# Layer-norm in three parts, gate copies between weight splits, and ScalarE weighing the last heads

## The chip, the cores and the metric

The kernel runs on one core of one Trainium2 chip. The metric is the device time in microseconds of one execution. Three runs of the kernel before gave 857.67, 858.05 and 861.17 us, so the median is 858.05 us.

## What is computed

`x` is 4 x 256 tokens of 512 numbers. The reference, cut to what matters:

```python
xn = _layernorm(x, axis=-1)                      # (x - mean) / sqrt(var + 1e-5)
s = _L0_attn_ref(xn, wq, wk, wv, wo)             # 32 query heads, 8 key heads, head 128, window 128, rope
g = _silu(_L0_ffn_ref(xn, w1, s1, w2, s2, w3, s3))
x = x + s * g
# _L0_ffn_ref: weights are packed 4-bit numbers, one scale for 64 of them
a = einsum('bsd,hd->bsh', x, W1); b = einsum('bsd,hd->bsh', x, W3)      # hidden 1376
h = _silu(a) * b; return einsum('bsh,dh->bsd', h, W2)
# _L0_attn_ref, for each head: scores, mask, softmax, times v, then @ wo
```

## The kernel before

Every large product is made of three products of rounded parts: an operand `w` is split into a high part `wh` (a copy to the rounded type, by ScalarE) and a low part `wl = w - wh` (by VectorE or GpSimd), and `three` (L1005) adds `sh*mh`, `sh*ml` and `sl*mh` in one PSUM bank. Each engine runs a list written out by hand, in order; semaphores tie the lists together.

**Start.** SyncE issues the loads (L223 to L230): the first packed weights `load13(0, 0)`, then rows 0 to 3 of `x` (a row tile is 128 tokens x 512), then more weights, then rows 4 to 7. VectorE dequantises the first weights (`dequant13(0, 0)`: `nib`, a shift of the packed numbers, and `W13`, a product with the scales). It then takes `bn_stats` of four rows, and `scales(0)` turns them into a mean and a reciprocal root in seven small steps, with ScalarE's square root (`root`) between. `norm_here` (VectorE) and `norm` (ScalarE) normalise rows. TensorE first spreads the scales of the first weights over the partitions (`scale_rows`, L1069), then transposes the normalised rows (`x_turn`, L1018), which ScalarE (`x_hi`) and VectorE (`x_lo`) split. `w13_start` (L1042) computes the first hidden tile in quarter pieces of 256 tokens, `w13_mult` in pieces of 512. The low part of the first four weights is made by GpSimd (`w13_first`), and `x_turn(4)` to `x_turn(7)` run inside and after `w13_mult(1, 0, 0)`. The second four rows are normalised by `scales(1)`. `PARTS` (L176) holds the two parts.

**FFN.** There are 11 hidden tiles of 128, `t` = 0 to 10. For each, TensorE computes `a` and `b` for two halves of the tokens (`w13_tile`), ScalarE applies silu, VectorE multiplies (`hid`), and both split the result. After each odd tile from 3 on, `w2_mult(u)` computes the second product of tiles 2u and 2u+1 for 8 token tiles, in 4 PSUM banks used in turn; tile `i` waits until tile `i-4` has been read. The reader is VectorE's `ffn_add(u)`, which copies (u = 0) or adds each token tile into `gate`. In VectorE's list it stands at the end of iteration `t = 2u+3` (L806 to L811), behind `w13_lo(t + 2, 0)` and `w13_lo(t + 2, 1)`, the low parts of the weights two tiles ahead.

**Attention.** The eight key heads (`g`) and two pairs of batches (`bp`) make 16 steps. In a step four query heads of two batches (`b` = 0, 1) go through `scores` (TensorE), `masking` (VectorE, with the row maximum), `exps` (ScalarE, with the row sum), `inverse` (a reciprocal) and `normalise` (VectorE multiplies the probabilities by it, 128 and then 256 columns, L855), `p_turn` (TensorE transposes them), `p_hi` and `p_lo` (split), `attend`, `o_hi` and `o_lo`, and `out_project`. Each head is prepared in the step before the one that uses it.

**End.** In the last step but one (`last`, `bp == 0`), VectorE prepares the four heads of batch 0 for the last step (L973 to L983): `finish(0, 0)`, `masking`, four `normalise`, and `finish(0, 1)` in between. In the last step the heads of batch 1 follow: VectorE normalises head 0, ScalarE (`weigh`, L546) heads 1 to 3. TensorE's last step (L1202 to L1216) is `p_turn` 0 and 1, `out_project(g, 0, 3)`, `p_turn` 2, `attend(0)`, and so on. `finish(bp, t)` multiplies a projected tile with the gate. GpSimd meanwhile runs `rest(t)` (two operations for each of 8 tiles) and `add_rest(t)`, and SyncE stores the tiles.

Of the kernel before, what the change touches and what calls it, by code (L numbers as in the profile page):

```python
# [20 lines left out]
GH = NQ // NKV  # L21
# [5 lines left out]
NT = TOK // P  # L27
DT = D // P
# [16 lines left out]
def build(nc, x, wq, wk, wv, wo, w13, s13, w2, s2, const, shifts, side, out):  # L45
# [10 lines left out]
    with ctx:  # L56
# [118 lines left out]

        PARTS = ((0, 1, 2, 3), (4, 5, 6, 7))  # L176

# [26 lines left out]
        def _(sp):  # L204
# [13 lines left out]
            def load2(t):  # L218
                wait(sp, W2_done, t - 1)
                sp.dma_start(pk2[:, t % 2, :], w2[t]).then_inc(w2_in[t % 2], 16)  # L220
                sp.dma_start(sc2[:, t % 2, :], s2[t]).then_inc(w2_in[t % 2], 16)

            load13(0, 0)  # L223
            for i in range(4):
                load_x(i)
            load13(0, 1)
            load13(1, 0)
            for i in range(4, NT):
# [175 lines left out]
        def _(act):  # L404
# [47 lines left out]
            nc.scalar.activation(warm[:, 1:2], warm[:, 0:1], ACT.Sqrt)  # L452
            w13_hi(0, 0)
            root(0)
            norm(1)
            for i in range(4):
                x_hi(i)
            w13_hi(0, 1)
            w13_hi(1, 0)
            root(1)  # L460
            nc.scalar.activation(warm[:, 2:3], warm[:, 0:1], ACT.Silu)
            w13_hi(1, 1)
            norm(5)
            norm(7)
            x_hi(4)
            x_hi(5)
# [124 lines left out]
            def step(g, bp, last):  # L591
# [4 lines left out]
                if not more:  # L596
                    p_hi(g, bp, 0, 0)
                    p_hi(g, bp, 0, 1)
                    exps(g, bp, 1, 2)
                    exps(g, bp, 1, 3)  # L600
                    weigh(g, bp, 1, 1)
                    p_hi(g, bp, 0, 2)
                    weigh(g, bp, 1, 2)
                    weigh(g, bp, 1, 3)
                    o_hi(g, bp, 0)
                    o_hi(g, bp, 1)
                    for r in range(3):
                        p_hi(g, bp, 1, r)
                    o_hi(g, bp, 2)
                    o_hi(g, bp, 3)  # L610
                    return
# [31 lines left out]
                kq_hi(ng, nbp, 4)  # L643
                for h in range(GH):
                    exps(ng, nbp, 0, h)
                if last:
                    exps(ng, nbp, 1, 0)
                    exps(ng, nbp, 1, 1)
                if nxt:
                    for c in range(6):  # L650
                        hi_in(g + 1, c)
# [11 lines left out]
        def _(dve):  # L663
# [4 lines left out]

            def scales(part):

# [6 lines left out]
                v, r0, r, t = [std[:, n, first:last] for n in (0, 1, 2, 3)]  # L677
                nc.vector.tensor_scalar(v, mv[:, first:last, 1], EPS, None, ALU.add).then_inc(ln_small, 1)
                dve.wait_ge(std_done, part + 1)
                nc.vector.reciprocal(r, r0).then_inc(ln_small, 1)  # L680
# [22 lines left out]

            def dequant13(t, m):

                s = t % 2
                dve.wait_ge(w13_in[s][m], 64 * (t // 2) + 32)
                if t < 2:
                    dve.wait_ge(sfirst_ps, 2 * t + m + 1)
                if 1 <= t <= 2:  # L710
                    dve.wait_ge(W13l_first, 2 * t + m - 1)
                wait(dve, W13_done, 2 * t + m)
                nc.vector.tensor_scalar(nib[:, m, :], pk[:, s, m, :], shc[:, 4:5], shc[:, 5:6],  # L713
                                        ALU.logical_shift_left, ALU.arith_shift_right).then_inc(nib_done, 1)
                dve.wait_ge(nib_done, 2 * t + m + 1)
                scale = bank[2 + 2 * t + m][:, :] if t < 2 else sc[:, s, m, :]
                nc.vector.tensor_tensor(W13[:, m, :], nib[:, m, :], scale, ALU.mult).then_inc(W13_done, 1)

            def w13_lo(t, m):
# [38 lines left out]

            nc.vector.memset(warm[:, :], 1.0).then_inc(warm_set, 1)
            dve.wait_ge(shift_in, 16)  # L760
            dequant13(0, 0)
            for i in range(4):
                stats(i)
            scales(0)
            norm_here(0)
            norm_here(2)
            norm_here(3)
            x_lo(0)
            x_lo(1)
            dequant13(0, 1)  # L770
            x_lo(2)
            x_lo(3)
            dequant13(1, 0)
            for i in range(4, NT):
                stats(i)
            scales(1)
            norm_here(4)
            norm_here(6)
            dequant13(1, 1)
            x_lo(4)  # L780
# [16 lines left out]
            for t in range(2, FT):  # L797
                if t + 2 < FT:
                    dequant13(t + 2, 0)
                hid(t, 0)  # L800
                if t + 2 < FT:
                    dequant13(t + 2, 1)
                dequant2(t - 1 if t < FT - 1 else t)
                if t == FT - 2:
                    dequant2(t)
                hid(t, 1)  # L806
                if t + 2 < FT:
                    w13_lo(t + 2, 0)
                    w13_lo(t + 2, 1)
                if t > 2 and t % 2:  # L810
                    ffn_add((t - 3) // 2)  # L811
            def cos_part(g, bp, c):
# [105 lines left out]
            def step(g, bp, last):  # L918
                ng, nbp = (g, 1) if bp == 0 else (g + 1, 0)
                more = not (last and bp == 1)  # L920
                if not more:
                    p_lo(g, bp, 0, 0)
                    p_lo(g, bp, 0, 1)
                    normalise(g, bp, 1, 0)
                    inverse(g, bp, 1, 1)
                    finish(0, 2)
                    inverse(g, bp, 1, 2)
                    finish(0, 3)
                    inverse(g, bp, 1, 3)
                    p_lo(g, bp, 0, 2)  # L930
# [42 lines left out]
                if last:  # L973
                    finish(0, 0)
                    masking(ng, nbp, 0, 2)
                    normalise(ng, nbp, 0, 0)
                    normalise(ng, nbp, 0, 1)
                    masking(ng, nbp, 1, 0)
                    normalise(ng, nbp, 0, 2)
                    normalise(ng, nbp, 0, 3)  # L980
                    finish(0, 1)
                    masking(ng, nbp, 1, 2)
# [21 lines left out]
        def _(pe):  # L1004
# [13 lines left out]
            def x_turn(i):  # L1018
                if i in (1, 5, 7):
                    pe.wait_ge(xn_done, (1, 5, 7).index(i) + 1)  # L1020
                else:
                    pe.wait_ge(xn_here, (0, 2, 3, 4, 6).index(i) + 1)
                wait(pe, xl_done, i - 3)
# [17 lines left out]

            def w13_start(m, part):  # L1042

# [4 lines left out]
                          [(W13h[:, 0, m, d, :], W13l[:, 0, m, d, :], xh[:, d, cols], xl[:, d, cols])  # L1048
                           for d in range(DT)])
                if part:  # L1050
# [26 lines left out]
            pe.wait_ge(id_in, 16)  # L1077
            for i in range(4):
                x_turn(i)
            scale_rows(1, 0)  # L1080
            scale_rows(1, 1)
            w13_start(0, 0)
            w13_start(0, 1)
            w13_mult(0, 0, 1)
            w13_mult(1, 0, 0, {3: lambda: x_turn(4)})
            for i in range(5, NT):
                x_turn(i)
            w13_mult(1, 0, 1)
# [242 lines left out]
```

## Time and profile before

| what | us |
|---|---|
| median of three runs | 858.05 |
| the profiled execution | 861.75 |
| its span (first to last instruction) | 859.9 |
| TensorE busy (matmul) | 834.0, 97% |
| VectorE busy | 610.6, 71% |
| ScalarE busy | 459.8, 53% |
| GpSimd busy | 394.7, 46% |

The profiled execution took 1.85 us more than its span, and 3.7 us more than the median of the three runs. TensorE's granted clock was 0.994 of full speed on average over it. TensorE is busy nearly all the time, so what counts is where it is not, and where its clock is low. The chain of work that ended last is 88% TensorE and 5% VectorE.

### The profile page before, as it was taken

Reading aid. Unit: us, or ns where it says so; the run is one execution under the profiler, and the core shown is the slowest. Engines: PE = TensorE matmul, PEld = TensorE weight load, DVE = VectorE, ACT = ScalarE, POOL = GpSimd, SP = SyncE. Lnnn points to the kernel's source line nnn. Section 1 sums busy time; section 2 is a strip of 40 time slices with the busy share of each in tenths; the row PEclk is TensorE's granted clock in tenths of the full one; section 3 lists DMA queues with packets and bytes.
Section 4 is the critical chain, followed back from the end, with each engine's and each line's share of the span. In section 5 each row is a group of like instructions: output and inputs, shape, how many; then the busy total and the mean of one; then the engine's idle time right before and its main releaser. Section 6 shows DMA issues by size and latency. Waiting matters only on the chain.

```text
span 859.9 us, 13737 instructions
## 1 busy us (share of the span) xinstructions
PE 834.0 (97%) x4140; PEld 695.4 (81%) x4140; DVE 610.6 (71%) x1626; ACT 459.8 (53%) x1133; POOL 394.7 (46%) x304
## 2 busy tenths in 40 slices
PE   6998999999889999999999999999999999999987
PEld 3887888888668888888888888888888888888865
DVE  6586667644678768785867687687858676876894
ACT  3431311313675747574855757475748557674842
POOL 1231312326365517453543655174535436641893
PEclk9999999999999999999999999999999999999989
DMA  7543322212012001201020120012010201200121
GB/s 209 159 120 101 104 74 69 63 48 74 2 49 69 7 1 50 74 2 36 13 73 0 49 63 10 0 49 73 0 34 15 73 0 49 63 10 1 49 63 74
DMA packets 43449, 44.48 MB, mean 52 GB/s; under 512 B 3476, under 2 KB 28182, under 8 KB 43414
## 3 DMA queue, kind: packets, MB, share of 16 engines
q1 hardware_dynamic: 43120, 43.99, 17.8%
q8 instruction: 17, 0.28, 0.1%
q14 instruction: 16, 0.13, 0.1%
q10 hardware_dynamic: 296, 0.09, 0.0%
HBM read 41.96 MB, written 2.10 MB: 51 GB/s over the span
## 4 chain that ended last, share of the span: by engine, by line
PE 88%; DVE 5%; issue 2%; ACT 2%; POOL 1%; DMA 0%; ACTq 0%; POOLq 0%; DVEq 0%
PE bank L1012 26%; PE bank L1014 26%; PE bank L1013 26%; PE bank L1148 5%; PE bank L1128 3%; DVE probs L855 1%; POOL acc L354 1%; PE bank L1118 1%; DVE W13l L721 1%; PE bank L1071 1%; PE bank L1025 1%; DVE nib L713 0%; DVE nib L737 0%; DVE act_h L730 0%; DVE probs L840 0%
## 5 line engine op out<-in xcount | busy, mean ns | idle before, releaser
L337 POOL TENSOR_TENSOR swap<-swap,cst 128x512 f32<-128x512 f32 x80 | 103.5, 1294 | 256.3 <-ACT swap L515 255.0
L1012 PE MATMUL bank<-xh,wih 128*128 128x512 f32 x384 | 158.0, 412 | 0.2 <-DVE q L819 0.2
L1014 PE MATMUL bank<-xh,wil 128*128 128x512 f32 x384 | 150.8, 393 | 0.0
L1013 PE MATMUL bank<-xl,wih 128*128 128x512 f32 x384 | 150.0, 391 | 0.0
L542 ACT ACTIVATE probs<-probs,nmx 128x128 f32<-128x128 f32 (+1 forms) x256 | 113.5, 445 | 36.6 <-DVE nmx L840 36.2
L855 DVE TENSOR_SCALAR probs<-probs,rinv 128x128 f32<-128x128 f32 x250 | 125.3, 543 | 4.4
L558 ACT ACTIVATE ph<-bank 128x512 fp32r<-128x512 f32 x96 | 55.7, 598 | 109.3 <-PE bank L1148 107.9
L1012 PE MATMUL bank<-woh,oh 128*128 128x512 f32 x256 | 101.0, 395 | 0.0
L1014 PE MATMUL bank<-woh,ol 128*128 128x512 f32 x256 | 100.5, 393 | 0.0
L1013 PE MATMUL bank<-wol,oh 128*128 128x512 f32 x256 | 100.5, 393 | 0.0
L861 DVE TENSOR_TENSOR pl<-bank,ph 128x512 fp32r<-128x512 f32 x96 | 64.7, 688 | 40.4 <-ACT ph L558 40.2
L341 POOL TENSOR_TENSOR q<-q,swap 128x512 f32<-128x512 f32 x64 | 89.1, 1392 | 8.1 <-DVE q L819 3.7
L1014 PEld LDWEIGHTS bank<-xh,wil 128*128 128x128 f32 x384 | 72.1, 188 | 16.1
L1012 PEld LDWEIGHTS bank<-xh,wih 128*128 128x128 f32 x384 | 72.4, 188 | 12.0 <-DVE q L819 0.7
L1013 PEld LDWEIGHTS bank<-xl,wih 128*128 128x128 f32 x384 | 72.5, 189 | 11.8
L321 POOL TENSOR_TENSOR wil<-raw,wih 128x512 fp32r<-128x512 f32 x48 | 61.0, 1307 | 42.1 <-ACT wih L497 42.1
L840 DVE CUSTOM_DVE_ANT_0 probs<-bank,cst 128x128 f32<-128x128 f32 (+1 forms) x256 | 76.4, 349 | 5.1 <-issue 5.1
L296 POOL TENSOR_TENSOR hl<-act_h,hh 128x512 fp32r<-128x512 f32 x22 | 31.1, 1416 | 95.1 <-ACT hh L439 95.1
L872 DVE TENSOR_TENSOR ol<-bank,oh 128x512 fp32r<-128x512 f32 x64 | 43.3, 687 | 40.4 <-ACT oh L563 40.4
L1012 PE MATMUL bank<-xh,W13h 128*128 128x512 f32 (+1 forms) x180 | 70.7, 393 | 0.0
L1014 PE MATMUL bank<-xh,W13l 128*128 128x512 f32 (+1 forms) x180 | 70.3, 391 | 0.0
L1013 PE MATMUL bank<-xl,W13h 128*128 128x512 f32 (+1 forms) x180 | 70.2, 390 | 0.0
(102 smaller groups left out, 1818.5 us busy)
## 6 DMA issues: line engine op xcount, KB each, us to landing
raw<-in_wq SPq DMA_DIRECT2D x32, 256.0 KB, 2.8
raw<-in_wo SPq DMA_DIRECT2D x32, 256.0 KB, 2.9
pk<-in_w SPq DMA_DIRECT2D x44, 128.0 KB, 3.7
sc<-in_s SPq DMA_DIRECT2D x36, 128.0 KB, 3.7
pk<-in_w SPq DMA_DIRECT2D x11, 256.0 KB, 2.7
sc<-in_s SPq DMA_DIRECT2D x11, 256.0 KB, 3.1
xn<-in_x SPq DMA_DIRECT2D x8, 256.0 KB, 4.3
raw<-in_wk SPq DMA_DIRECT2D x8, 256.0 KB, 3.2
```

The source lines that it names most:

```text
L321: nc.gpsimd.tensor_tensor(lo, raw[:, slot, :], hi.bitcast(f32), ALU.subtract).then_inc(wl_done, 1)
L337: nc.gpsimd.tensor_tensor(v, v, spread(sin.unsqueeze(1), P, 2, SEQ), ALU.mult).then_inc(sin_done, 1)
L341: nc.gpsimd.tensor_tensor(dst, dst, swap[:, s, :], ALU.add).then_inc(rope_done, 1)
L542: e = nc.scalar.activation(probs[:, s, c0:c1], probs[:, s, c0:c1], ACT.Exp, bias=nmx[:, s, i:i + 1], scale=-1.0, accum_out=rsum[:, s, i:i ...
L558: nc.scalar.activation(ph[:, r, :], T_B[(7 * bp + j) % 2][:, :], ACT.Copy).then_inc(ph_done, 1)
L840: m = nc.vector.tensor_tensor_reduce(out=probs[:, s, c0:c1], in0=S_B[s % 2][:, c0:c1], in1=mask[:, c0:c1], scale=-SM, scalar=TOP, op0=ALU. ...
L855: m = nc.vector.tensor_scalar(probs[:, s, c0:c1], probs[:, s, c0:c1], rinv[:, s, i:i + 1], None, ALU.mult)
L861: nc.vector.tensor_tensor(pl[:, r, :], T_B[(7 * bp + 4 * b + r) % 2][:, :], ph[:, r, :].bitcast(f32), ALU.subtract).then_inc(pl_done, 1)
L872: nc.vector.tensor_tensor(ol[:, j].rearrange("p h n -> p (h n)"), O_B[j % 2][:, :], oh[:, j].rearrange("p h n -> p (h n)").bitcast(f32), A ...
L1012: nc.tensor.matmul(out_, sh, mh, start=(i == 0), stop=False)
L1013: nc.tensor.matmul(out_, sh, ml, start=False, stop=False)
L1014: m = nc.tensor.matmul(out_, sl, mh, start=False, stop=(i == n - 1))
```

## The change

Start: `PARTS` is now three parts, rows 0 and 1, rows 2 and 3, rows 4 to 7. SyncE loads rows 0 and 1 ahead of the first weights, and rows 2 and 3 behind the second. `scales` takes a piece of work (`between`) that VectorE does while ScalarE takes the root: the shift `nib13` of a weight. Dequantising is cut in `nib13` and `scale13`. Row 3 is normalised by ScalarE instead of VectorE. TensorE turns two rows, runs the first quarter of both first weights, and turns rows 2 and 3 inside the second.

FFN: `ffn_add` is cut in three: tiles 0 and 1 ahead of `w13_lo(t + 2, 0)`, tiles 2 and 3 between the two, tiles 4 to 7 behind.

End: the four heads of batch 0 in the last step but one, and head 0 of batch 1 in the last, are weighed by ScalarE; VectorE gives only the reciprocals.

```diff
-        PARTS = ((0, 1, 2, 3), (4, 5, 6, 7))
+        PARTS = ((0, 1), (2, 3), (4, 5, 6, 7))
 # SyncE
+            load_x(0)
+            load_x(1)
             load13(0, 0)
-            for i in range(4):
-                load_x(i)
             load13(0, 1)
+            load_x(2)
+            load_x(3)
             load13(1, 0)
 # ScalarE
-            w13_hi(0, 0)
             root(0)
             norm(1)
-            for i in range(4):
-                x_hi(i)
+            x_hi(0)
+            w13_hi(0, 0)
+            x_hi(1)
             w13_hi(0, 1)
+            root(1)
+            norm(3)
+            x_hi(2)
+            x_hi(3)
             w13_hi(1, 0)
-            root(1)
+            root(2)
             nc.scalar.activation(warm[:, 2:3], warm[:, 0:1], ACT.Silu)
-            w13_hi(1, 1)
             norm(5)
             norm(7)
+            w13_hi(1, 1)
...
                     p_hi(g, bp, 0, 1)
+                    weigh(g, bp, 1, 0)
                     exps(g, bp, 1, 2)
...
-                for h in range(GH):
-                    exps(ng, nbp, 0, h)
-                if last:
+                if last and bp == 0:
+                    exps(ng, nbp, 0, 0)
+                    exps(ng, nbp, 0, 1)
+                    exps(ng, nbp, 0, 2)
+                    weigh(ng, nbp, 0, 0)
+                    exps(ng, nbp, 0, 3)
+                    weigh(ng, nbp, 0, 1)
+                    weigh(ng, nbp, 0, 2)
+                    weigh(ng, nbp, 0, 3)
                     exps(ng, nbp, 1, 0)
                     exps(ng, nbp, 1, 1)
+                else:
+                    for h in range(GH):
+                        exps(ng, nbp, 0, h)
 # VectorE
-            def scales(part):
+            def scales(part, between):
...
                 nc.vector.tensor_scalar(v, mv[:, first:last, 1], EPS, None, ALU.add).then_inc(ln_small, 1)
+                between()
                 dve.wait_ge(std_done, part + 1)
...
+            stats(0)
+            stats(1)
             dve.wait_ge(shift_in, 16)
-            dequant13(0, 0)
-            for i in range(4):
-                stats(i)
-            scales(0)
+            scales(0, lambda: nib13(0, 0))
             norm_here(0)
-            norm_here(2)
-            norm_here(3)
+            scale13(0, 0)
+            stats(2)
             x_lo(0)
+            stats(3)
             x_lo(1)
             dequant13(0, 1)
+            scales(1, lambda: nib13(1, 0))
+            norm_here(2)
+            scale13(1, 0)
+            stats(4)
             x_lo(2)
             x_lo(3)
-            dequant13(1, 0)
-            for i in range(4, NT):
-                stats(i)
-            scales(1)
+            stats(5)
+            stats(6)
+            stats(7)
+            scales(2, lambda: nib13(1, 1))
             norm_here(4)
             norm_here(6)
-            dequant13(1, 1)
+            scale13(1, 1)
...
                 hid(t, 1)
+                second_product = t > 2 and t % 2
+                if second_product:
+                    ffn_add((t - 3) // 2, range(2))
                 if t + 2 < FT:
                     w13_lo(t + 2, 0)
+                if second_product:
+                    ffn_add((t - 3) // 2, range(2, 4))
+                if t + 2 < FT:
                     w13_lo(t + 2, 1)
-                if t > 2 and t % 2:
-                    ffn_add((t - 3) // 2)
+                if second_product:
+                    ffn_add((t - 3) // 2, range(4, NT))
...
-                    normalise(g, bp, 1, 0)
+                    inverse(g, bp, 1, 0)
                     inverse(g, bp, 1, 1)
                     finish(0, 2)
                     inverse(g, bp, 1, 2)
+                    inverse(g, bp, 1, 3)
                     finish(0, 3)
-                    inverse(g, bp, 1, 3)
...
                     masking(ng, nbp, 0, 2)
-                    normalise(ng, nbp, 0, 0)
-                    normalise(ng, nbp, 0, 1)
+                    for h in range(GH):
+                        inverse(ng, nbp, 0, h)
+                    finish(0, 1)
                     masking(ng, nbp, 1, 0)
-                    normalise(ng, nbp, 0, 2)
-                    normalise(ng, nbp, 0, 3)
-                    finish(0, 1)
                     masking(ng, nbp, 1, 2)
 # TensorE
-            for i in range(4):
-                x_turn(i)
+            x_turn(0)
+            x_turn(1)
             scale_rows(1, 0)
+            w13_start(0, 0)
             scale_rows(1, 1)
-            w13_start(0, 0)
+            w13_start(1, 0, {2: lambda: x_turn(2), 3: lambda: x_turn(3)})
             w13_start(0, 1)
-            w13_mult(0, 0, 1)
-            w13_mult(1, 0, 0, {3: lambda: x_turn(4)})
-            for i in range(5, NT):
-                x_turn(i)
+            w13_start(1, 1)
+            w13_mult(1, 0, 0, {2: lambda: x_turn(4), 3: lambda: x_turn(5)})
+            x_turn(6)
+            x_turn(7)
```

## Rows read from the trace of the kernel before

**Rows 1.** Waits of TensorE: instruction, releaser: us in total, times, longest us.

```profile
PE bank L1148 <- DVE probs L855: 5.7, 3, 3.3
PE bank L1025 <- DVE xn L695: 4.4, 1, 4.4
PE bank L1012 <- DVE gate L754: 2.4, 1, 2.4
```

**Rows 2.** Windows: us from and to, length, busy us of each engine, granted clock (PEclk).

```profile
11.87:24.47 12.60, 12.60 (x45) 9.72 (x46) 10.87 (x27) 5.59 (x10) 2.54 (x2) 1.00 0.76 204
...
75.67:79.09 3.42, 3.42 (x9) 2.65 (x8) 1.89 (x4) 0.00 (x0) 0.00 (x0) 0.50 0.38 95
224.70:261.00 36.30, 29.46 (x157) 23.59 (x156) 26.63 (x85) 26.81 (x68) 19.65 (x16) 1.00 0.10 30
...
831.15:836.84 5.69, 5.69 (x18) 4.82 (x19) 5.38 (x19) 3.47 (x12) 5.53 (x5) 0.50 0.51 153
```

**Rows 3.** Timeline of SyncE's queue, start: us, us long, instruction, count.

```profile
0.75 1.21 SPq L213 DMA_DIRECT2D pk<-in_w  x2
```

**Rows 4.** DMA issues from 1.99 to 2.4: size, median us to landing.

```profile
xn<-in_x SPq DMA_DIRECT2D x1, 256.0 KB, 3.6
```

**Rows 5.** Timeline of VectorE, start: in brackets the idle time before and its releaser.

```profile
7.08 2.46 DVE L667 BATCH_NORM_STATS2 stat<-xn 128x6 f32<-128x512 f32 x4
...
15.08 0.54 DVE L713 TENSOR_SCALAR nib<-pk,shc 128x512 int32<-128x512 int32 x1
...
17.61 1.02 DVE L713 TENSOR_SCALAR nib<-pk,shc 128x512 int32<-128x512 int32 x1
```

**Rows 6.** Timeline of TensorE, start.

```profile
11.87 3.65 PE L1025 MATMUL bank<-cst,xn 128*128 128x128 f32 x16 [4.41 <-DVE xn L695]
...
24.22 0.40 PE L1014 MATMUL bank<-xh,W13l 128*128 128x256 f32 x1
...
24.44 0.42 PE L1012 MATMUL bank<-xh,W13h 128*128 128x512 f32 x1
```

**Rows 7.** Timeline of GpSimd, start.

```profile
17.08 1.26 POOL L287 TENSOR_TENSOR W13l<-W,W13h 128x512 fp32r<-128x512 f32 x1 [7.91 <-ACT W13h L425]
```

**Rows 8.** Timeline of VectorE from 70 us.

```profile
70.60 0.69 DVE L730 TENSOR_TENSOR act_h<-act_h,bank 128x512 f32<-128x512 f32 x1 [1.19 <-ACT act_h L432]
...
72.51 1.97 DVE L721 TENSOR_TENSOR W13l<-W,W13h 128x512 fp32r<-128x512 f32 x2 [1.22 <-ACT W13h L425]
74.39 2.47 DVE L754 COPY gate<-bank 128x512 f32<-128x512 f32 x4
```

**Rows 9.** Timeline of TensorE at 75 us.

```profile
75.13 0.50 PE L1012 MATMUL bank<-W2h,hh 128*128 128x512 f32 x1 [2.41 <-DVE gate L754]
```

**Rows 10.** All of line 855: count, ns min/median/max, first and last start.

```profile
L855 DVE TENSOR_SCALAR probs<-probs,rinv x250: 285/347/1423, 233.7 to 834.8; 128x128 f32<-128x128 f32 x125
```

**Rows 11.** Timeline of VectorE, end.

```profile
823.30 2.50 DVE L855 TENSOR_SCALAR probs<-probs,rinv 128x128 f32<-128x128 f32 x2
...
828.71 2.38 DVE L855 TENSOR_SCALAR probs<-probs,rinv 128x128 f32<-128x128 f32 x2
...
838.76 0.69 DVE L861 TENSOR_TENSOR pl<-bank,ph 128x512 fp32r<-128x512 f32 x1 [0.30 <-ACT ph L558]
```

**Rows 12.** ScalarE's groups from 827 to 845: busy us, mean ns, idle before.

```profile
L542 ACT ACTIVATE probs<-probs,nmx 128x256 f32<-128x256 f32 (+1 forms) x7 | 3.1, 449 | 0.0
L558 ACT ACTIVATE ph<-bank 128x512 fp32r<-128x512 f32 x5 | 2.9, 599 | 5.3 <-PE bank L1148 5.3
L550 ACT ACTIVATE probs<-probs,rinv 128x128 f32<-128x128 f32 (+1 forms) x6 | 2.3, 445 | 0.8 <-DVE rinv L848 0.8
```

**Rows 13.** Timeline of TensorE, end.

```profile
831.15 1.97 PE L1148 MATMUL bank<-cst,probs 128*128 128x128 f32 x8 [3.31 <-DVE probs L855]
...
839.60 0.47 PE L1012 MATMUL bank<-ph,vh 128*128 128x512 f32 x1 [0.81 <-DVE pl L861]
```

**Rows 14.** Timeline of GpSimd, end.

```profile
839.96 1.30 POOL L358 TENSOR_TENSOR acc<-acc,raw 128x512 f32<-128x512 f32 x1
```

More of the change, by code:

```diff
@@ L702, in x_lo, with nib13, scale13 @@
                                         xh[:, :, cols].bitcast(f32), ALU.subtract).then_inc(xl_done, 1)
-            def dequant13(t, m):
+            def nib13(t, m):
                 s = t % 2
                 dve.wait_ge(w13_in[s][m], 64 * (t // 2) + 32)
+                wait(dve, W13_done, 2 * t + m)
+                nc.vector.tensor_scalar(nib[:, m, :], pk[:, s, m, :], shc[:, 4:5], shc[:, 5:6],
+                                        ALU.logical_shift_left, ALU.arith_shift_right).then_inc(nib_done, 1)
+            def scale13(t, m):
+                s = t % 2
                 if t < 2:
@@ L711, in dequant13 @@
                     dve.wait_ge(W13l_first, 2 * t + m - 1)
-                wait(dve, W13_done, 2 * t + m)
-                nc.vector.tensor_scalar(nib[:, m, :], pk[:, s, m, :], shc[:, 4:5], shc[:, 5:6],
-                                        ALU.logical_shift_left, ALU.arith_shift_right).then_inc(nib_done, 1)
                 dve.wait_ge(nib_done, 2 * t + m + 1)
@@ L717, in dequant13 @@
                 nc.vector.tensor_tensor(W13[:, m, :], nib[:, m, :], scale, ALU.mult).then_inc(W13_done, 1)
+            def dequant13(t, m):
+                nib13(t, m)
+                scale13(t, m)
             def w13_lo(t, m):
@@ L1018, in x_turn @@
             def x_turn(i):
[L1019 to L1022, printed above, removed]
+                pe.wait_ge(xn_done if i % 2 else xn_here, i // 2 + 1)
                 wait(pe, xl_done, i - 3)
@@ L1040, in w13_mult, with w13_start @@
                        for d in range(DT)], ahead).then_inc(ab_ps, 1)
-            def w13_start(m, part):
+            def w13_start(m, part, ahead=None):
                 cols = slice(2 * part * P, (2 * part + 2) * P)
@@ L1048, in w13_start @@
                           [(W13h[:, 0, m, d, :], W13l[:, 0, m, d, :], xh[:, d, cols], xl[:, d, cols])
-                           for d in range(DT)])
+                           for d in range(DT)], ahead)
                 if part:
```

## Prediction

> **What bounds the kernel now.** I read the page's busy shares first: TensorE has work for 97% of the span, so only its waits and its clock can give time back. The waits of TensorE [rows 1] name three releasers that the change touches: 4.4 us for the first normalised row, 2.4 us for the first read of a gate bank, and 5.7 us in three waits for weighed probabilities, the longest of them 3.3. Then I took windows for the clock [rows 2]. Two stretches stand at half the full level, that is at 1.2 GHz instead of 2.4: 3.42 us right after the gate wait and, after the 3.3 us wait near the end, the 5.69 us in which TensorE next worked. The first window of rows 2 reads 1.00, but its instructions say otherwise: the last product of 256 columns takes 0.40 and the next, of 512, takes 0.42 [rows 6], and 16 turns took 3.65, 0.23 each, as the 8 in 1.97 did in the stretch at 0.50 [rows 13]. So the start too ran at 1.2 GHz, until 24.4 us; the products of 256 columns there follow each other in 0.22 [rows 6], which is about 0.12 at the full level. A microsecond of TensorE work at that level costs half a microsecond.
>
> The profiled execution took 861.75 us, 3.7 above the median of 858.05. The two late stretches at the low level are worth about 1.7 + 1.5 us (below) and would explain most of that. I therefore make the sum twice: against the profiled execution with them, and against the median without them.
>
> **Start.** Moved ahead: rows 0 and 1, their statistics and their seven small steps. Added: a third set of small steps on VectorE (about 1.3 us), and `nib13` before each reciprocal. Today the four statistics end at 9.54 [rows 5] and TensorE's first turn comes at 11.87 [rows 6], 2.3 later. Now the queue's first issue, at 0.75 [rows 3], is row 0; a row landed 3.6 after its issue [rows 4], which gives 4.4, and 4.9 to 5.2 for row 1. Two statistics at 0.62 [rows 5] end at about 5.8. To the 2.3 come a shift of 0.54 [rows 5], and two aggregations fewer take away 0.2: the first turn starts at 8.5 instead of 11.87. It can't be before 7.46, where the wait of 4.41 begins [rows 6], and with landings a microsecond later it is 9.5.
>
> What comes back of these 3.4 us? Until 24.47 TensorE did 12.6 us of work, all at the low level [rows 2]: 16 turns, two scale spreads, 24 products of 256 columns. The new order does the same work, with about 0.65 of new waits in it (for the low part of the first weight, made by GpSimd in 1.26 [rows 7] behind ScalarE's copy, and for the low part of row 3), so it is there at 8.5 + 0.65 + 12.6 = 21.7. What follows up to the end of the first hidden tile's first half is 24 products of 256 columns, where 12 of 512 stood; on columns that is equal. If the clock rises at 24.47 as before, 12 or 13 of them cost 0.22 and the rest 0.12, ending at 25.8 instead of 27.2: gain 1.4. If it rises at the same point of the work, 2.7; but then the fourth first weight, ready at about 29.3 by VectorE's list, is later than TensorE and holds the gain at 2.2. I take **2.0**, and the bounds -1 (rows land 1 us later and the level rises 3 us later than today) and 3.4. VectorE's extra small steps fall in time that it has: it idles 2.4 us before it needs the result of the third half tile, at 40 us.
>
> One row speaks against this part. The same shift took 1.02 instead of 0.54 when GpSimd was making a low part [rows 5, 7], and the new order puts shifts and norms beside that work. The Trainium skill's SBUF — State Buffer, section "Who interferes with whom", says VectorE and GpSimd share one port pair, held by one of them for a whole instruction. By it the first weights would come up to 0.5 us later and the start's gain would be about 1.5; the 2.0 and its bounds stand without it.
>
> **Gate copies.** Today VectorE ends `hid(3, 1)` at 71.29, splits two weights until 74.48 and only then copies [rows 8]. TensorE wanted bank 0 back at 75.13 - 2.41 = 72.72 [rows 9]. Now two copies at 0.62 follow `hid` at once: the first bank is free at 71.9, 0.8 before it is wanted; the second at 72.5, wanted 1.37 later than the first (six products of 0.23). One split, about 1 us, then the copies of tiles 2 and 3, done at 74.1 and 74.8, wanted at 75.4 and 76.8. No wait is left. The splits come up to 4 us later, but serve tile 5, which is 20 us away. So 2.41 goes, and with it the low stretch behind it, 3.42 at half level [rows 2], 1.7: **4.1** against the profile, **2.4** against a run whose clock did not fall there. The three later `ffn_add` calls cause no wait today, and I cost them at nothing: TensorE's list, not VectorE, is late there. Were the 0.8 of cover used up by a late silu, each microsecond would cost one. Bounds 1.5 and 4.1. The shift by the start does not use this cover: VectorE's chain to 71.29 hangs on TensorE's result at 40 us and moves with it.
>
> **Last heads.** Beside GpSimd's `rest` work two halves of a head took 2.50 and 2.38 on VectorE [rows 11], where the median piece is 0.35 [rows 10]. Four heads held VectorE for 8.5 us, and TensorE, ready at 827.84, started the turns at 831.15 [rows 13]. On ScalarE an exp pair is 0.90 and a weighing pair 0.89 busy, 0.74 when they follow each other [rows 12]. ScalarE has the third exp done at 821.5, then one exp pair and four weighings: 821.5 + 0.9 + 4 x 0.74 = 825.3. That is 2.5 before 827.84, so the 3.31 goes in full. VectorE, freed, masks the next heads earlier than today.
>
> What is late next: in the last step ScalarE must now do, between `p_hi(0, 1)` (done 829.45) and `p_hi(0, 2)`, one weighing more. VectorE gives its reciprocal at 830.4, behind two `p_lo`. Then weigh 0.8, two exp pairs 1.8, weigh 0.74: 833.7; `p_hi` 0.60 [rows 12], `p_lo` 0.69 [rows 11]: 835.1. TensorE, through with the turns, the projection and the first part of `attend` at 832.5, waits 2.6 there, where today it waits 0.81 and starts at 839.60 [rows 13]. Then it is TensorE's own list to the end, as today. Gain 839.60 - 835.1 = **4.5** against the profile. Without the low stretch today's wait would end at 838.1, because VectorE's slow weighing of the fifth head and ScalarE's pieces behind it end last: so that stretch was worth 1.5, and the gain is **3.0** against a run without it. GpSimd's last `rest` ends at 841.26 [rows 14] and its result is wanted only by the last tiles, after 848; it binds nothing. Bounds: 0.5 (the new wait of 2.6 brings as long a low stretch, 5.69 us, as today's profile has, where today's run has none) and 4.5.
>
> **The sum.** Profiled: 861.75 - 2.0 - 4.1 - 4.5 = 851.2. Median: 858.05 - 2.0 - 2.4 - 3.0 = 850.7. The new wait of 2.6 can itself bring the low level (the 2.41 did; in the first attention step 6.84 us of shorter waits in 36.3 left the clock at 1.00 [rows 2]); at an even chance of 1.7 that adds 0.8 to the second. I say **851.3**.
>
> **Rivals.**
> A (forecast, 0.64): all three pay, 849 to 853.
> B (0.13): the start gives nothing. For it: the clock may rise no earlier, and the first weights now arrive behind rows. Against: the rows land well before VectorE is free of other work. 858.05 - 2.4 - 3.0 + 0.8 = 853.5.
> C (0.12): at the end the wait only moves to ScalarE and the clock falls with it. For it: the 2.6 computed above. Against: 3.31 and 0.81 are gone. Then the end gives 0 to 0.5: 853.5 to 854.5.
> D (0.06): the copies don't do what they say, because `hid(3, 1)` comes over 0.8 late and the wait moves instead of going; with a start of 1 this is 855.
> E (0.05), slower: the clock. TensorE's first work now alternates turns, scale spreads, quarter products and short waits; if that keeps it at 1.2 GHz, every microsecond beyond 24.4 costs half of one. The rest of the sum, 6.8, is gone if it stays low until 38 us, and 0.5% is lost from 47 us on; until 52 us the time is 851.3 + 13.8 = 865. Against: the first attention step, which alternates in the same way.
>
> **Numbers.** A measurement of this kernel can't tell less than 0.5%, 4.3 us, from no change. Faster than 853.8: A, half of B and C: 0.77. Within: the rest of B and C, and D: 0.19. Slower than 862.3: most of E, 0.04. The range of 8 in 10 reaches down to 848.5 (858.05 - 3.4 - 2.4 - 3.0 is 849.2, and 0.7 if some runs of before have the low stretch at 76 us) and up to 855.0, which takes in B, C and most of D.
>
> **What would show it.** First turn at 8 to 9.5 us; the first product of 512 columns spaced 0.23 by 22 to 25 us; no wait of TensorE for L754, and a granted clock of 1.00 from there on; 10 pieces fewer on L855 and 10 more of `weigh`; a first turn of the last step right behind the scores; a new wait of about 2.6 before the second part of `attend`, released by `p_lo`. Wrong would be: a start that reaches 40 us of old work no earlier, TensorE waiting for W13l or for a row's low part by over a microsecond, or the last turns waiting for ScalarE.

## The result, and the profile after

The changed kernel takes 850.99 us (median of 5 runs, 847.94 to 852.83), the kernel before beside it 860.1 (median of 5, 857.67 to 861.5). The ratio is 0.9899 with a 95% interval of 0.9877 to 0.9920, so the change gives about 8.7 us, 6.9 to 10.6. The forecast was 851.3, within 848.5 to 855.0. The profiled execution after took 847.94 and is the fastest of its five, the one before took 861.75 and is slower than any of its five. So the 13.8 us between the two profiles are more than the change gives, and the sections below keep the two apart.

The page after, its first lines and the granted clock in 40 slices. Its first digit reads 9 although TensorE's products before 15 us ran at 1.2 GHz by their lengths (below), so at the start I go by lengths and not by this row:

```profile
span 846.1 us, 13773 instructions
...
PE 827.1 (98%) x4152; PEld 690.7 (82%) x4152; DVE 600.5 (71%) x1621; ACT 463.2 (55%) x1145; POOL 394.9 (47%) x304
...
PEclk9999999999999999999999999999999999999999
```

The waits of TensorE after, which answer to [rows 1]:

```profile
PE bank L1045 <- DVE pl L896: 3.1, 2, 2.3
PE bank L1179 <- DVE probs L890: 2.4, 2, 1.8
...
PE bank L1055 <- DVE xn L712: 0.4, 1, 0.4
```

The wait for a gate copy is gone. That for the first row fell from 4.4 to 0.4 us. Of the 5.7 for weighed probabilities 2.4 are left, in two waits of the first attention step, which the change does not touch. The 2.3 for `pl`, ahead of the second part of `attend`, is new in this size: 0.81 stood there [rows 13].

TensorE's timeline after, at the start, answers to [rows 6]:

```profile
8.11 1.94 PE L1055 MATMUL bank<-cst,xn 128*128 128x128 f32 x8 [0.39 <-DVE xn L712]
...
14.50 0.41 PE L1047 MATMUL bank<-xh,W13l 128*128 128x256 f32 x1
...
16.18 0.28 PE L1046 MATMUL bank<-xl,W13h 128*128 128x256 f32 x1
...
19.67 0.36 PE L1045 MATMUL bank<-xh,W13h 128*128 128x256 f32 x1 [1.15 <-DVE xl L718]
...
62.52 0.39 PE L1045 MATMUL bank<-W2h,hh 128*128 128x512 f32 x1
```

The first turn comes at 8.11, where 11.87 stood. The length of a product of 256 columns falls from 0.41 to 0.28 between 14.5 and 16.2: there the clock rises to 2.4 GHz, 9 us sooner than before. The last row is the FFN's second product, which began at 67.11 before.

The wait of 1.15 at 19.67 is new: it is for the low part of row 3. VectorE's and GpSimd's timelines show most of it arise earlier:

```profile
13.98 1.04 DVE L699 TENSOR_TENSOR std<-std 128x2 f32<-128x2 f32 x1
```

```profile
13.73 1.27 POOL L289 TENSOR_TENSOR W13l<-W,W13h 128x512 fp32r<-128x512 f32 x1 [2.04 <-ACT W13h L427]
```

A small step on two columns took 1.04 here, where the same step had taken 0.16 seven microseconds before. It ended at 15.02, as GpSimd's low part of a weight did (15.00), and rows 2 and 3 are normalised behind it.

VectorE's timeline after, around the gate copies, answers to [rows 8]:

```profile
66.01 0.69 DVE L755 TENSOR_TENSOR act_h<-act_h,bank 128x512 f32<-128x512 f32 x1 [1.18 <-ACT act_h L434]
66.61 1.28 DVE L779 COPY gate<-bank 128x512 f32<-128x512 f32 x2
67.92 1.38 DVE L746 TENSOR_TENSOR W13l<-W,W13h 128x512 fp32r<-128x512 f32 x1
69.22 1.28 DVE L779 COPY gate<-bank 128x512 f32<-128x512 f32 x2
```

Two copies, a split, two copies: the first bank is free at 67.3, and TensorE came to it at 67.98 without a wait.

The end after: ScalarE's groups from 811 to 826 (busy, mean ns, idle before), which answer to [rows 12], then TensorE's timeline, which answers to [rows 13].

```profile
L556 ACT ACTIVATE probs<-probs,rinv 128x128 f32<-128x128 f32 (+1 forms) x16 | 6.0, 443 | 0.9 <-DVE rinv L883 0.9
L548 ACT ACTIVATE probs<-probs,nmx 128x128 f32<-128x128 f32 (+1 forms) x12 | 5.3, 442 | 0.9 <-DVE nmx L875 0.9
```

```profile
818.58 1.04 PE L1179 MATMUL bank<-cst,probs 128*128 128x128 f32 x8
...
825.84 0.47 PE L1045 MATMUL bank<-ph,vh 128*128 128x512 f32 x1 [2.33 <-DVE pl L896]
```

Of these sixteen pieces of `weigh` ten are the moved ones. The mean is 0.44, as for ScalarE's own pieces before (445 ns, [rows 12]). The turns follow the scores at once.

### The profile page after: what moved, and what is told of

The parts are those of the page before. It is cut to its first block, busy times and chain, and to the rows that moved or that the text cites. A ratio compares the mean times of both kernels' runs of the same rounds, so it can differ in the third digit from the quotient of the medians.

```text
span 846.1 us, 13773 instructions
## 1 busy us (share of the span) xinstructions
PE 827.1 (98%) x4152; PEld 690.7 (82%) x4152; DVE 600.5 (71%) x1621; ACT 463.2 (55%) x1145; POOL 394.9 (47%) x304
## 4 chain that ended last, share of the span: by engine, by line
PE 93%; DVE 3%; ACT 2%; issue 1%; DMA 0%; POOL 0%; SPq 0%; ACTq 0%
PE bank L1045 28%; PE bank L1047 28%; PE bank L1046 28%; PE bank L1179 5%; PE bank L1159 3%; DVE probs L890 1%; PE bank L1149 1%; PE bank L1055 1%; DMA pk<-in_w 0%; DVE probs L875 0%; PE bank L1101 0%; DVE ql L861 0%; DVE pl L896 0%; DVE ol L907 0%; ACT probs L548 0%
## 5 line engine op out<-in xcount | busy, mean ns | idle before, releaser
L890 DVE TENSOR_SCALAR probs<-probs,rinv 128x128 f32<-128x128 f32 x240 | 115.2, 522 | 4.3
L896 DVE TENSOR_TENSOR pl<-bank,ph 128x512 fp32r<-128x512 f32 x96 | 64.6, 687 | 40.5 <-ACT ph L564 40.5
```

The lines of the kernel that those rows point to most:

```text
L890: m = nc.vector.tensor_scalar(probs[:, s, c0:c1], probs[:, s, c0:c1], rinv[:, s, i:i + 1], None, ALU.mult)
L896: nc.vector.tensor_tensor(pl[:, r, :], T_B[(7 * bp + 4 * b + r) % 2][:, :], ph[:, r, :].bitcast(f32), ALU.subtract).then_inc(pl_done, 1)
```

## The experiments

To tell the parts apart I read three stretches of each profile: when TensorE begins the FFN's second product (the start), how long it takes from there to the fifth hidden tile (the gate copies), and from there to its last product (mostly the end). The experiments ran in three groups, each on one chip with the kernel before beside it: there it took 859.49 (the three parts alone, new end with new start 848.77), 859.12 (the change again, copies and heads with the old start, new end with old start 847.90, GpSimd's rest work cut down) and 858.8 (the others). Numbers of different groups are compared with that in mind.

| kernel | median us | second product at | to the fifth tile | to the last product |
|---|---|---|---|---|
| before | 858.8 to 860.1 | 67.11 | 15.18 | 773.3 |
| start alone | 857.59 | 65.91 | 13.59 | 773.6 |
| gate copies alone | 853.47 | 67.15 | 10.89 | 771.2 |
| last heads alone | 856.97 | 67.18 | 15.19 | 768.6 |
| GpSimd's rest work cut down, on before | 852.14 | 64.60 | 13.61 | 766.6 |
| all three (the change) | 850.99 | 62.52 | 10.90 | 768.5 |
| the change again | 851.26 | 65.44 | 10.89 | 770.3 |
| copies and heads, old start | 852.01 | 66.57 | 10.89 | 768.5 |
| new end, new start | 848.77, 848.71 | 65.40, 63.45 | 10.89, 10.89 | 766.3, 766.2 |
| new end, old start | 847.90, 848.27 | 66.64, 67.04 | 10.89, 10.89 | 766.2, 766.2 |
| new end, old start, extra products | 846.59 | 63.21 | 10.89 | 766.3 |
| the change, first copies behind a split | 850.68 (1 run) | 63.07 | 13.05 | 768.5 |

**Start alone.** The hunks of the diff on `PARTS`, the loads, `scales`, the norms, `nib13` and `scale13`, and the order of turns and first products; nothing else.

```diff
-        PARTS = ((0, 1, 2, 3), (4, 5, 6, 7))
+        PARTS = ((0, 1), (2, 3), (4, 5, 6, 7))
...
```

> Only the start part of the change; gate copies and last heads as before. Two theories of why the start gave 4.6 us between the two profiles where 2.0 was forecast. Theory A: the new order runs 12 products of 256 columns in one train from 12 us on, and the clock rises behind it (15.1 us in the profile after, 24.5 before); then the rise stands before 19 us here too, the second product of the FFN begins 3.5 to 4.6 us earlier than the 67.1 of before, and the time is 3.5 to 5 us under before. Rival B: where the clock rises is chance; then the rise can be anywhere up to 25 us, the median gain is about 2 and the runs spread over 3 us. Both: the wait for the gate copy (2.4) and for the last heads (3.3) are still there.

857.59 (12 runs, 856.25 to 860.40) against 859.49 (24 runs, 856.00 to 862.08), ratio 0.9986, interval 0.9970 to 1.0002: 1.2 us by the ratio, 1.9 by the medians, and zero is just inside. Its waits show that the other two are still there:

```profile
PE bank L1165 <- DVE probs L874: 5.7, 3, 3.3
...
PE bank L1031 <- DVE gate L769: 2.4, 1, 2.4
```

The turns at 20.5 us still took 1.05 for four, which take 0.60 at the full level, so the clock had not risen 19 us in: theory A fell. The second product came 1.2 sooner.

**Gate copies alone.**

```diff
                 hid(t, 1)
+                second_product = t > 2 and t % 2
+                if second_product:
+                    ffn_add((t - 3) // 2, range(2))
                 if t + 2 < FT:
                     w13_lo(t + 2, 0)
...
```

> Only the gate copies are spread between the weight splits. Forecast theory: the wait of 2.4 for the gate copy goes, with no other wait in its place, and so does the low clock behind it: 2.4 to 4.1 us under before. Rival: VectorE is late anyway and the wait moves to a later tile or to the low parts of the weights two tiles on: under 1 us. The start is as before, so its clock rise is one more sample of the old order: theory A of the start says 22 us or later, rival B anywhere.

853.47 (7 runs, 852.70 to 855.61), ratio 0.9938, interval 0.9916 to 0.9960: 5.3 us, 3.4 to 7.2. No wait for a gate copy is left and none came in its place. The stretch in the table went from 15.18 to 10.89, 4.3 us, where the clock had fallen behind the wait, and from 13.6 to 10.9, 2.7, where it had not (start alone, and the cut rest work). The median gives more than either, with an interval that holds the 4.3 but not the 2.7. The profiled execution, 855.42, is not typical of this kernel: five of its seven runs took 852.70 to 853.67, so the stretches above are those of a slow run.

**Last heads alone.**

```diff
-                    normalise(g, bp, 1, 0)
+                    inverse(g, bp, 1, 0)
...
+                    weigh(g, bp, 1, 0)
...
```

> Only the last heads are weighed by ScalarE. Forecast theory: the wait of 3.3 ahead of the last turns goes, a wait of about 2.3 to 2.6 comes ahead of the second part of attend where 0.8 stood: 3.0 us under a run of before without a low clock there, 4.5 under one with it. Rival: ScalarE becomes what ends last and the gain is under 1 us. The start is as before: one more sample of the old order's clock rise.

856.97 (12 runs, 854.02 to 858.42), ratio 0.9970, interval 0.9951 to 0.9989: 2.6 us, 0.9 to 4.2. The 3.3 us wait is gone from its waits, and the new one stands where it was forecast:

```profile
834.98 0.47 PE L1020 MATMUL bank<-ph,vh 128*128 128x512 f32 x1 [2.33 <-DVE pl L871]
```

**GpSimd's rest work cut down,** on the kernel before. It leaves out the gate product and the residual of all columns but one.

```diff
-                nc.gpsimd.tensor_tensor(acc[:, t, :], acc[:, t, :], gate[:, t, :], ALU.mult)
+                nc.gpsimd.tensor_tensor(acc[:, t, 0:1], acc[:, t, 0:1], gate[:, t, 0:1], ALU.mult)
...
```

> The kernel before, with GpSimd's rest work near the end cut to one column of 512 in both of its operations (it leaves out the gate product and the residual of the other columns). VectorE weighs all last heads, as before. Theory: the 2.1 to 2.5 us of a head are VectorE waiting for GpSimd; then a pair of pieces on line 855 takes about 0.55, the four heads are weighed some 5 us sooner, and the 3.3 us wait of TensorE ahead of the last turns goes to under 0.5, so that the time is 3 us under before. Rival: VectorE's list, its masks and ScalarE's exps are what is late; then the pieces stay over 0.8 each or the wait stays over 2.

852.14 (5 runs) against 859.12. VectorE's weighing of the last heads, in its timeline:

```profile
816.50 0.55 DVE L855 TENSOR_SCALAR probs<-probs,rinv 128x128 f32<-128x128 f32 x2
817.16 0.55 DVE L855 TENSOR_SCALAR probs<-probs,rinv 128x128 f32<-128x128 f32 x2
...
820.29 0.55 DVE L855 TENSOR_SCALAR probs<-probs,rinv 128x128 f32<-128x128 f32 x2
```

0.55 in all four heads, where [rows 11] have 2.50 and 2.38, and TensorE's first turn follows the scores at once (823.12). So the long pieces came from GpSimd's work beside them, as the forecast took them. The Trainium skill's SBUF — State Buffer, section "Who interferes with whom", says that VectorE in one of its two-port modes and GpSimd keep each other out for a whole instruction. The durations agree with that (two pieces took 2.50 beside operations of GpSimd of 1.28 and 1.29, and 0.55 where those were cut down); in which mode these pieces ran no run shows. The median fell by 7 and not by 3, which has other parts in it. In its profile the clock also rose early, near 16 us (the second product came at 64.60, with the old start), it did not fall behind the wait for the gate copy (13.61), and at the end the wait ahead of the second part of `attend` stayed at 0.81, since ScalarE got no more to weigh: its last stretch is 2.0 shorter than that of last heads alone.

**The end in another order** (with the whole change).

```diff
 # ScalarE, last step but one, then last step
                     exps(ng, nbp, 1, 1)
+                    weigh(ng, nbp, 1, 0)
+                    weigh(ng, nbp, 1, 1)
...
-                    weigh(g, bp, 1, 0)
                     exps(g, bp, 1, 2)
+                    p_hi(g, bp, 0, 2)
                     exps(g, bp, 1, 3)
-                    weigh(g, bp, 1, 1)
-                    p_hi(g, bp, 0, 2)
...
 # VectorE: inverse(1, 0) and (1, 1) ahead of masking(1, 2); p_lo(0, 2) behind inverse(1, 2)
 # TensorE
-                    out_project(g, 0, 3)
-                    p_turn(g, bp, 0, 2, True)
+                    out_project(g, 0, 3, ahead={2: lambda: p_turn(g, bp, 0, 2, True)})
```

> The changed kernel with the end put in another order: ScalarE weighs heads 0 and 1 of batch 1 in the 1.4 us in which it idles before the last step (VectorE gives their reciprocals before the last masks), the third copy of the turned probabilities comes right behind one exp pair, and TensorE turns that block inside the projection instead of behind it. Forecast theory: the 2.3 us wait ahead of the second part of attend is nothing but ScalarE's list, so it goes down to 0 to 0.5 and the time is about 2 us under the changed kernel (849 for 851). Rival: the wait only moves to the turns of batch 1 or to finish(0, 3), which attend also waits for, and the gain is under 0.7 us.

848.77 (6 runs, 848.42 to 850.60), 10.7 under the kernel before on the same chip (859.49), where the change is 8.7 under its own by the ratio. Where the changed kernel waits 2.33, TensorE now starts 0.48 behind the instruction before it:

```profile
826.06 0.40 PE L1047 MATMUL bank<-ph,vl 128*128 128x512 f32 x1
826.54 0.50 PE L1045 MATMUL bank<-ph,vh 128*128 128x512 f32 x1
```

The last stretch of the table falls from 768.5 to 766.3, 2.2 us. So the order of the lists was all of the new wait. The edit moves steps on ScalarE, VectorE and TensorE at once, so ScalarE's share of it is not shown by itself.

**The change again.**

> The changed kernel once more, as the measure for the others of this job. The first profile showed the clock's rise at 15.1 us, the start part alone had it at 22.0, the reordered end at 20.5, while three profiles of the old start had it at 24.5 to 24.7. Theory B: the rise is a matter of chance within 15 to 22 us in the new order, so here it can be anywhere in that span; the median is 850 to 852 and the runs spread over 4 us.

851.26 (6 runs, 848.37 to 852.89). The second product came at 65.44, not at 62.52 as in the first profile. Here the clock also fell behind the new wait. Two stretches of TensorE's end by windows (the last three figures of a row are the granted clock, the share of DMA and its GB/s): 1.00 falls to 0.53, near 1.2 GHz.

```profile
826.00:830.10 4.10, 1.76 (x8) 1.18 (x7) 1.76 (x5) 3.94 (x13) 3.94 (x4) 1.00 0.47 154
830.10:833.50 3.40, 3.40 (x15) 2.89 (x14) 2.38 (x4) 1.79 (x3) 3.40 (x3) 0.53 0.40 110
```

It cost 770.3 - 768.5 = 1.8 us, the 1.7 that the forecast gave an even chance.

**The change without its start.** The start hunks undone.

```diff
-        PARTS = ((0, 1), (2, 3), (4, 5, 6, 7))
+        PARTS = ((0, 1, 2, 3), (4, 5, 6, 7))
...
```

> The changed kernel with the start as before (old load order, two parts, old order of turns and products); gate copies and last heads as changed. Theory of the forecast: the start is worth 2.0, the time is 852.5 to 853.5 and the second product of the FFN begins at 67.1. Rival C: the start alone gave 1.9 with an interval that reaches zero, and it gives nothing where the clock would have been high anyway: under 0.8 slower than the changed kernel. Rival A (clock rises far earlier): over 3 slower.

852.01 (6 runs, 850.55 to 852.46) beside 851.26 on the same chip: 0.75 slower. By its own line, under 0.8, this is rival C.

**The reordered end with the old start,** timed twice, the second time beside the same kernel with the new start.

```diff
-        PARTS = ((0, 1), (2, 3), (4, 5, 6, 7))
+        PARTS = ((0, 1, 2, 3), (4, 5, 6, 7))
...
```

> The reordered end with the start as before. The same pair once more, without a wait over 0.5 us near the end: against the reordered end (848.8) 2 slower by the forecast's theory, under 0.8 by rival C.

> The reordered end with the new start, again, beside its twin with the old start on the same chip. Forecast's theory: 2 under the twin. Rival C: within 1 of it, because the old start's longer train of turns lets the clock rise early in more of its runs, which gives back what the rows gain.

> The reordered end with the old start, again: 847 to 850, two or more groups of runs 2 to 3 us apart (early and late rise of the clock).

847.90 and 848.27 with the old start, 848.77 and 848.71 with the new. The new start is not faster in either pair (the first is of two chips). Yet its second product comes sooner in its profiles: at 65.4 to 65.9 in three and 62.5 to 63.5 in three, against 66.6 to 67.2 in six profiles with the old start and 64.6 in one.

The times of the single runs say how both can be so. The four profiled executions of the reordered end differ only in the start, since their other two stretches agree within 0.1. Each row is one profile and the six runs beside it:

| start | profiled run | second product at | runs of 848.0 or less |
|---|---|---|---|
| new, late rise | 848.65 | 65.40 | 0 of 6 |
| new, early rise | 846.64 | 63.45 | 2 of 6 |
| old, late rise | 849.85 | 66.64 | 4 of 6 |
| old, late rise | 850.24 | 67.04 | 3 of 6 |

With a late rise in both the new start is 1.2 to 1.6 faster, as the second product shows. But the two profiles with the old start are of the slowest runs of their six, and 7 of its 12 runs, against 2 of 12, took 848.0 or less, where of the four profiled ones only the one with the early rise did. So with the old start the clock seems to rise early more often. No trace of those quick runs is kept, and this is argued from times alone.

**Extra products in the first wait,** on the reordered end with the old start.

```diff
+            nc.gpsimd.memset(hl[:, 0, 0:IT + P].bitcast(f32), 1.0).then_inc(fill_set, 1)
...
+            pe.wait_ge(fill_set, 1)
+            for n in range(10):
+                nc.tensor.matmul(bank[7][:, :], hl[:, 0, IT:IT + P], hl[:, 0, 0:IT], start=True, stop=True)
             pe.wait_ge(id_in, 16)
```

> The reordered end with the old start, and ten extra products of 128x128 by 512 columns of ones into a bank that nobody reads, put where TensorE waits 4.4 us for the first normalised row (between the first two scale spreads and the first turn). They leave the result alone. Theory B': the start's time hangs on where the clock rises, which is late (23 to 25 us) in most runs and early (15 to 16) in some, and on little else; then the extra products bring the rise to under 16 us in every run, the FFN's second product begins at 64 to 64.6 instead of 66.6, the median falls by 1 to 2.5 under the same kernel without them and its slowest runs vanish. Forecast's theory (the first row's arrival decides): the rise may move, but with the rows as late as before the gain stays under 0.5.

846.59 (6 runs, 846.43 to 847.07) beside 848.27 (846.46 to 850.24): the fastest kernel of the study, 0.9856 of before with an interval of 0.9828 to 0.9885, and its runs spread over 0.6 us where the twin's spread over 3.8. TensorE's timeline:

```profile
7.20 4.25 PE L1095 MATMUL bank<-hl 128*128 128x512 f32 x10
11.68 1.94 PE L1041 MATMUL bank<-cst,xn 128*128 128x128 f32 x16 [0.23 <-DVE xn L707]
```

The sixteen turns took 1.94 where they took 3.65 [rows 6]: they ran at the full level from the first. The second product came at 63.21. The ten products stand where TensorE waited anyway. That the second product didn't come sooner still has its reason in the rows: TensorE now waits for one of the second four, where the old start with a late rise had no such wait.

```profile
26.10 1.53 PE L1041 MATMUL bank<-cst,xn 128*128 128x128 f32 x12 [1.57 <-ACT xn L414]
```

**The first copies behind a split** (on the change).

```diff
-                if second_product:
-                    ffn_add((t - 3) // 2, range(2))
                 if t + 2 < FT:
                     w13_lo(t + 2, 0)
                 if second_product:
-                    ffn_add((t - 3) // 2, range(2, 4))
+                    ffn_add((t - 3) // 2, range(4))
```

> The changed kernel with the first two gate copies put behind the first weight split instead of ahead of it. Forecast's arithmetic: the cover was 0.8 and a split takes about 1 (up to 1.4 beside GpSimd), so a wait of TensorE for the gate copy of 0.2 to 0.6 comes back at the fifth tile, and no more. Rival: VectorE has slack there and nothing comes back, or the whole 2.4 does.

A miss. The wait that came back is 1.82, three to nine times what I expected. VectorE's timeline, then TensorE's:

```profile
66.58 0.69 DVE L755 TENSOR_TENSOR act_h<-act_h,bank 128x512 f32<-128x512 f32 x1 [1.18 <-ACT act_h L434]
68.49 1.36 DVE L746 TENSOR_TENSOR W13l<-W,W13h 128x512 fp32r<-128x512 f32 x1 [1.22 <-ACT W13h L427]
```

```profile
70.50 0.50 PE L1043 MATMUL bank<-W2h,hh 128*128 128x512 f32 x1 [1.82 <-DVE gate L779]
```

The split costs not only its 1.36: it waits 1.22 for ScalarE's high part first, the same 1.22 that stands in [rows 8]. The two copies of the change fill just that idle time.

## Why the prediction was right

**In total** it was right, and in part by luck. It forecast a gain of 6.75 from a median of three runs, 858.05; with five runs that median is 860.1, and the gain is 8.7, its interval (6.9 to 10.6) just above the forecast. The time came out because the two differences cancel. The order of the parts was not right either: by experiments the gate copies gave most, the heads next and the start little.

**Gate copies, forecast 4.1 with the clock's fall and 2.4 without.** Shown, by the stretch alone: 4.3 and 2.7. No wait followed. The first bank was free 0.7 before it was wanted, forecast 0.8. But the working took a split for about 1 us and left out that it first waits 1.22 for ScalarE [rows 8]; with the copies behind a split that gave the 1.82 where 0.2 to 0.6 was expected. The medians of copies alone and of heads with copies (856.97 to 852.01) give 5.3 by the ratio and 5.0, some 1 us more than the 4.3 and over 2 more than the 2.7. The first is within the interval; what the rest is stays open, and an earlier rise in more of the runs is possible but not shown.

**Last heads, forecast 4.5 and 3.0.** The last stretch shows 773.3 - 768.5 = 4.8 against a profile with the long low stretch, and 771.2 - 768.5 = 2.7 against one (copies alone) with a shorter. The medians show 2.6 for the heads on the kernel before, and 1.5 on top of the copies (853.47 to 852.01, two chips; 2.4 by the ratios). Every profile with the 3.3 us wait has a low stretch behind it, so the 3.0 without one was never measured by itself. That GpSimd made the pieces long is shown by the cut rest work. The new wait of 2.33 is the forecast 2.6, with the cause that it named, and its cost by the clock was seen once, at 1.8.

**Start, forecast 2.0.** This is the term that was mis-sized. The step down to the first turn held: forecast 8.5, measured 8.11. What did not hold is that the gain would come out at the end. Where the clock rose late in both orders the second product came 1.2 (65.91 for 67.11) to 1.7 us sooner (0.7 to 1.8 over all such pairs of profiles), about the 1.4 that the working gave for an unmoved rise, but the medians of four pairs give 1.9, 0.75, -0.9 and -0.4 for the start: 0.3 on average, and nothing that these runs can tell from zero. I had set the rise at one place for each order (24.47, or "the same point of the work"). It is not one place: with the old start it stood between 23 and 25 us in six profiles and near 16 in a seventh, where the second product came 2.5 sooner; with the new one near 15 to 17 in three and past 20 in three. That spread, about 3 us in when the second product begins, is larger than the term itself. That the rise decides more than the first row is shown by the extra products: the rows come as late as before, and the start is the fastest of all but two profiles, both of the new order with an early rise (62.52 and 63.07). The rows still bind behind it, with the 1.57. That the old start's long train of turns brings an early rise more often than the new order's mixed one is only argued from the pairs and the single runs' times.

One of the forecast's own signs of being wrong did show: TensorE waits over a microsecond for a row's low part, 1.15 in the first profile and 0.86 to 1.15 in the other five with the new start. The working had 0.65 for all new waits. It had feared that shifts and norms would be slow beside GpSimd's low parts; the shifts kept their 0.55, and a small step of two columns took 1.04 or 1.05 in all six profiles.

**The rivals.** E, the clock staying low, did not occur: the products were at the full level by 23.2 us in every profile with the new start. B, the start giving nothing, was true or nearly so, and the copies made up for it. C came true in part: a wait of 2.3 came where 0.81 stood and 3.3 went, and in the second profile the clock fell behind it, but even there the last stretch is 3.0 shorter than before (770.3 for 773.3). D did not occur: no profile of the change has a wait for a gate copy.

## What to carry to other kernels

Where TensorE waits, look at what its clock does behind the wait: here 2.41 us of waiting cost 4.3 in one execution and 2.7 in another, and which it is changes from run to run, so a single profile can over- or understate a change by 2 to 5 us. Before work is moved ahead of a wait, look for what the instructions behind are themselves waiting for: the copies were free because they stood in 1.2 us in which VectorE waited for ScalarE. Where an engine's pieces take several times their usual length, look at which engine works beside them, leave that work out once to see whether the pieces shrink, and then give them to an engine whose own pieces keep their length there. Where runs of one kernel fall in groups, see in which group the profiled run lies before two profiles are compared.

## What the runs showed of the hardware

Ten products that nobody reads, 4.25 us at the half level in a wait that was there anyway, made the sixteen turns behind them take 1.94 instead of 3.65 and drew the runs together from a spread of 3.8 us to 0.6. I had looked at the start as a chain of arrivals; it is as much a question of what TensorE does while it waits.

A step of VectorE on two columns took 1.04 where it takes 0.16, and ended with the instruction of GpSimd beside it (15.02 and 15.00). The size of a step says nothing of what it can cost beside another engine's work.

After waits of nearly one length the clock sometimes fell and sometimes did not: behind 2.4 us in the profile before and in heads alone (15.2 to the fifth tile), not in start alone and in the cut rest work (13.6); behind 2.33 in the second profile of the change (1.8 us lost), not in the first.
